# Two-layer decoder on one core: top-k attention in 56 full tiles instead of 64, a laid-out convolution kernel, and gating, norms and biases placed elsewhere

## The chip, the cores and the metric

The kernel runs on one core of one Trainium2 chip, all in float32, in one launch. The time is the device time of the slowest core in microseconds; with one core that is the core's own. TensorE (PE) multiplies matrices, VectorE (DVE), ScalarE (ACT) and GpSimd (POOL) work on rows of up to 128 partitions, and SyncE (SP) issues the transfers. All operands lie in on-chip memory as [partitions x columns]; matmul results go to eight PSUM banks of 2 KB a partition.

## The reference, cut to what matters

The input x is (16, 112, 256), the context (16, 375, 192). Each of six parts is added to x and the sum normalised:

```python
x = _layernorm(x + _L0_attn_ref(x, ...))       # selective scan, 16 sequences of 112
x = _layernorm(x + _L0_xattn_ref(x, ctx, ...)) # softmax cross-attention, 16 heads of 16
x = _layernorm(x + _L0_ffn_ref(x, ...))        # gate, best 2 of 8 experts, 256 -> 256 -> 256
x = _layernorm(x + _L1_attn_ref(x, ...))       # 4 encoder layers over the 16 rows of a position, FFN 1024
x = _layernorm(x + _L1_xattn_ref(x, ctx, ...)) # the part below
x = _layernorm(x + _L1_ffn_ref(x, ...))        # 3 cycles of a coupling network
```

The fifth part is the one that the change touches most (4 heads of 32, K_TOP = 32, here T = 112 rows and G = 375 context positions a batch):

```python
scores = einsum('bthd,bghd->bhtg', Q, K) / sqrt(DH)
scores = where(vision_mask, scores, -inf)
topv, topi = top_k(scores, 32);  probs = softmax(topv)
attn_mean = zeros.at[..., topi].set(probs).mean(axis=1)     # over the 4 heads
c_t = (attn_mean @ V) * text_mask
x = layernorm(x_text, g_norm_in, b_norm_in)
x = x * (1 + gate * scale_in) + gate * shift_in             # both from c_t @ W_film_in
y = causal convolution of x with a kernel of 112 lags for each of 256 features, + D_skip * x
y = y * (1 + gate * scale_out) + gate * shift_out           # both from c_t @ W_film_out
xt = x_text + y;  h = layernorm(xt, g_ffn, b_ffn);  xt = xt + gelu(h @ W1 + b1) @ W2 + b2
return layernorm(xt, g_norm_out, b_norm_out)
```

## The kernel before, in words

Each stage is a set of functions, one for each engine (`xat_pe`, `moe_dve`, `s4x_act` and so on), and each engine runs its functions in the order in which they are written. Semaphores alone tie the engines together, so an instruction that waits holds up everything behind it on its engine. The stages by their start in the trace: selective scan 0 us, cross-attention 333, gating and experts 651, encoder 914, the fifth part 1793, coupling network 2410.

**Cross-attention** (`xat_*`) runs in slots, a pair of heads each: scores L858, exponential, weighted values L871 and L891, and at the end of a batch its sums and its output projection (L901, L910, L919, added to the residual at L1045). Four batches are a quarter; at a quarter's end its rows are normalised (statistics L265 and L268, a root on GpSimd L285, application L277) and turned to features (L936). **Gating** comes after the last quarter: 64 TensorE instructions L1120 for all 16 batches, the two best experts on VectorE (L1196 to L1209), the weights turned at L1126 and copied at L1213. **Experts**: 32 steps (quarter, expert) of hidden L1137 and output L1158, added to the rows at L1224 with the weight of the gate.

**Encoder**: at its start the residual rows are turned back (L1293) in seven rounds, GpSimd adds a bias to each (L1639) and then builds the expanded queries (L1658) for the scores L1349.

**Top-k attention** (`s4x_*`): for each of 16 batches keys L1906, then for each of 4 heads a tile of 112 rows x 375 scores in a PSUM bank: L1917 contracts over the head's 32 features, in rows 32h to 32h+31 of the array, and L1919 adds the mask row with the same 32 rows. VectorE takes tiles in pairs: four rounds of MAX8 (L2158) and MATCH_REPLACE8 (L2167) mark the 32 best, ScalarE has meanwhile made the exponential (L2102), and L2177 keeps the marked ones and sums them. For each batch L2180 and L2181 give 1/sum, ScalarE makes a scaled diagonal of it for each head (dg, L2111), and L1928 multiplies the probabilities by it, which turns them and adds the heads up; L1937 gathers the context, L1946 makes c_t for each quarter. TensorE's order is keys(b+1), scores(b+1), then the context of b.

**Convolution**: the rows are normalised and modulated (L1969 for scale and shift, L2198, L2199), flipped in time by 8 matmuls with a reversed identity (L1983) and copied to x_r (L2118). Then 16 "taps" of 16 features each: 16 Toeplitz matrices of 112 x 112 are read from DRAM (rows of 448 bytes at overlapping addresses of a padded kernel) into 8 buffers (L1856, L1861), and L1996 multiplies each by the rows of 16 batches of one feature (32 columns, two features); L2006 turns the result. Scale and shift out, and the feed-forward part with L2052, follow for each quarter.

Quoted, the lines that set TensorE's order in the top-k stage:

```python
for b in range(B):
    if b + 1 < B:
        keys(b + 1)
        scores(b + 1)
    context(b)
    if b % QB == QB - 1:
        values(b // QB)
```

## Time and profile before

| what | value |
|---|---|
| median of 3 runs | 2531.08 us (2530.32 to 2533.37) |
| the profiled execution's own time | 2530.24 us |
| its span | 2528.4 us |
| mean granted TensorE clock | 0.883 |
| PE, DVE, ACT, POOL busy | 85%, 61%, 28%, 31% |
| chain that ended last, by engine | PE 62%, DVE 22%, POOL 6%, ACT 3% |
| moved by DMA | 101.68 MB, mean 40 GB/s |

The span runs from the first instruction to the last of the core. A program matmul in float32 shows as two instructions in the trace (x4 in a row of the trace are two matmuls of the program). A granted clock of 1.0 is TensorE at 2.4 GHz, 0.5 is 1.2 GHz, and a value between them is a stretch with both. In the program's names wc, wb, XD, XF, enc_w are storage used by several stages, so that a row's name can be that of an earlier owner.

### The profile page before, as it was taken

Reading aid. Unit: us, or ns where it says so; the run is one execution under the profiler, and the core shown is the slowest. Engines: PE = TensorE matmul, PEld = TensorE weight load, DVE = VectorE, ACT = ScalarE, POOL = GpSimd, SP = SyncE. Lnnn points to the kernel's source line nnn. Section 1 sums busy time; section 2 is a strip of 40 time slices with the busy share of each in tenths; the row PEclk is TensorE's granted clock in tenths of the full one; section 3 lists DMA queues with packets and bytes.
Section 4 is the critical chain, followed back from the end, with each engine's and each line's share of the span. In section 5 each row is a group of like instructions: output and inputs, shape, how many; then the busy total and the mean of one; then the engine's idle time right before and its main releaser. Section 6 shows DMA issues by size and latency. Waiting matters only on the chain.

```text
span 2528.4 us, 37624 instructions
## 1 busy us (share of the span) xinstructions
PE 2141.5 (85%) x15316; PEld 1493.9 (59%) x15316; DVE 1547.5 (61%) x3090; ACT 708.1 (28%) x1355; POOL 772.8 (31%) x707
## 2 busy tenths in 40 slices
PE   7888889999799978999999999887667775869886
PEld 2333457777566657878788787775445453336532
DVE  7998845555233325555656565575499896636546
ACT  6544333333112112222222222221222221211132
POOL 3334259876000034433444334332200001201101
PEclk8777789998699989999999999998767676879988
DMA  4212272221100010001001001000421111220001
GB/s 146 86 52 92 87 155 71 59 67 39 54 1 1 1 80 1 1 2 65 1 1 65 1 1 49 1 1 1 106 65 37 28 28 31 48 56 1 0 1 29
DMA packets 63597, 101.68 MB, mean 40 GB/s; under 512 B 32361, under 2 KB 56930, under 8 KB 62210
## 3 DMA queue, kind: packets, MB, share of 16 engines
q1 hardware_dynamic: 63426, 99.28, 13.8%
q8 instruction: 122, 2.00, 0.3%
q14 instruction: 49, 0.40, 0.1%
HBM read 78.77 MB, written 20.50 MB: 39 GB/s over the span
## 4 chain that ended last, share of the span: by engine, by line
PE 62%; DVE 22%; POOL 6%; ACT 3%; issue 3%; SPq 2%; DMA 2%; POOLq 0%; DVEq 0%; ACTq 0%
PE PS L1404 8%; PE PS L1420 8%; PE PS L1158 4%; DVE top L2158 4%; PE PS L1137 3%; DVE w_s L2167 3%; PE PS L1321 3%; PE PS L2043 2%; DVE ln_st L265 2%; PE PS L871 2%; PE PS L858 2%; PE PS L1349 2%; PE PS L1379 2%; PE PS L1431 2%; PE PS L404 2%
## 5 line engine op out<-in xcount | busy, mean ns | idle before, releaser
L284 POOL TENSOR_SCALAR ln_ve<-ln_mv 128x2 f32<-128x2 f32 (+1 forms) x91 | 20.9, 229 | 1309.4 <-DVE ln_mv L268 1309.3
L1596 DVE TENSOR_TENSOR p_x<-PS,cols 128x1024 f32<-128x1024 f32 x112 | 129.3, 1216 | 148.0 <-PE PS L1366 147.9
L1658 POOL TENSOR_TENSOR q_x<-q_f,cols 128x2048 f32<-128x2048 f32 x56 | 208.7, 3746 | 7.7 <-ACT q_f L1516 7.7
L1016 DVE TENSOR_REDUCE XD<-PS 112x2 f32<-112x750 f32 x128 | 120.1, 940 | 112.1 <-PE PS L858 111.9
L1224 DVE SCALAR_TENSOR_TENSOR XA<-PS,gate_w,XA 112x256 f32<-112x256 f32 x128 | 61.9, 484 | 133.7 <-PE PS L1158 133.7
L1928 PE MATMUL PS<-dg,e_p 112*125 112x112 f32 x384 | 82.5, 409 | 70.3 <-ACT dg L2111 70.3
L452 PE MATMUL PS<-bc_parts,ident 96*128 96x448 bf16 x256 | 106.0, 518 | 42.2 <-DVE st_h L686 28.9
L858 PE MATMUL PS<-enc_w,q_s 32*112 32x375 f32 x512 | 132.6, 544 | 4.7 <-DVE XD L1016 4.7
L984 ACT ACTIVATE e_t<-PS 125x672 f32<-125x672 f32 x128 | 93.5, 731 | 152.2 <-PE PS L871 152.2
L1486 ACT ACTIVATE wb<-PS,cols 128x256 f32<-128x256 f32 x224 | 90.8, 472 | 140.1 <-PE PS L1404 140.1
L1928 PEld LDWEIGHTS PS<-dg,e_p 112*125 112x125 f32 x384 | 79.3, 321 | 82.4 <-issue 82.4
L871 PE MATMUL PS<-q_s,enc_w 32*125 32x112 f32 x1536 | 124.2, 293 | 2.6 <-ACT e_t L984 2.6
L642 DVE TENSOR_TENSOR_SCAN st_h<-dA,st_h 128x3584 f32<-128x3584 f32 x16 | 121.0, 7606 | 0.0
L1158 PE MATMUL PS<-wc,h_t 128*112 128x256 f32 x512 | 117.5, 384 | 2.4 <-DVE XA L1227 2.4
L1404 PE MATMUL PS<-wc 128*128 128x256 f32 x448 | 104.4, 393 | 10.3 <-ACT wc L1531 10.3
L1158 PEld LDWEIGHTS PS<-wc,h_t 128*112 128x112 f32 x512 | 91.4, 179 | 32.4 <-issue 14.3
L1404 PE MATMUL PS<-wc,enc_w 128*128 128x256 f32 x448 | 100.4, 382 | 9.5 <-ACT wc L1531 9.5
L871 PEld LDWEIGHTS PS<-q_s,enc_w 32*125 32x125 f32 x1536 | 103.1, 193 | 8.0 <-issue 7.9
L741 POOL TENSOR_TENSOR st_h<-st_h 128x448 f32<-128x448 f32 x64 | 71.2, 1134 | 109.9 <-DVE st_h L686 109.9
L1404 PEld LDWEIGHTS PS<-wc 128*128 128x128 f32 x448 | 86.8, 196 | 26.0 <-ACT wc L1531 14.0
L1137 PE MATMUL PS<-XF,wc 128*128 128x448 f32 x256 | 101.4, 540 | 0.7 <-DVE gate_wt L1213 0.7
L2167 DVE MATCH_REPLACE8 w_s<-top,w_s 112x375 f32<-112x375 f32 x192 | 100.9, 533 | 0.0
(352 smaller groups left out, 4749.7 us busy)
## 6 DMA issues: line engine op xcount, KB each, us to landing
v_all_scratch<-v_st SPq DMA_DIRECT2D x16, 750.0 KB
v_t<-v_all_scratch SPq DMA_DIRECT2D x16, 750.0 KB
t_ring<-k_scratch SPq DMA_DIRECT2D x8, 784.0 KB, 11.9
enc_w<-in_enc_w SPq DMA_DIRECT2D x2, 3072.0 KB, 11.0
wc<-in_enc_w SPq DMA_DIRECT2D x2, 3072.0 KB, 11.5
k_all_scratch<-k_st SPq DMA_DIRECT2D x16, 375.0 KB
enc_w<-k_all_scratch SPq DMA_DIRECT2D x64, 93.8 KB, 3.6
ctx_k<-in_ctx SPq DMA_DIRECT2D x16, 281.2 KB
```

Source lines behind the costliest of these rows:

```text
L642: dve.tensor_tensor_scan(h, dA[:, n, :, :].rearrange("p n b t -> p (n b t)"), h, 0.0, ALU.mult, ALU.add).then_inc(scan_done, 1)
L858: ins = pe.matmul(ps[2 * (n % 2) + a][0:T, 0:S2], q_s[h, m, b * T:(b + 1) * T], k_s[h, b % 3, m, :], start=True, stop=True)
L871: ins = pe.matmul(ps[4 + a][0:JR, j * T:(j + 1) * T], k_s[h, b % 3, m, j * JR:(j + 1) * JR], q_s[h, m, b * T:(b + 1) * T], start=True, sto ...
L1016: dve.tensor_reduce(nm_w[0:T, g % 4, 64 * half + 16:64 * half + 49:32], PS[0:T, 2 * half:2 * half + 2, 0:S2], AX.X, ALU.max, negate=True). ...
L1137: last = pe.matmul(ps[pair + m][:, 0:QT], w1_e[:, e, k, m * P:(m + 1) * P], XF[:, k, q * QT:(q + 1) * QT], start=(k == 0), stop=(k == KC - 1))
L1158: last = pe.matmul(bank, h_t[:, i % 2, k, b * T:(b + 1) * T], w2_e[:, e, k, :], start=(k == 0), stop=(k == KC - 1))
L1404: last = pe.matmul(ps[bank][:, (m % 2) * RT:(m % 2 + 1) * RT], w[:, k, m * P:(m + 1) * P], x1f[:, i % 2, k, :], start=(k == 0), stop=(k == ...
L1420: last = pe.matmul(ps[3][:, g * D:(g + 1) * D], h_ff[:, m, g * P:(g + 1) * P], w[:, m, :], start=(m == 0), stop=(m == 7))
L1596: last = dve.tensor_tensor(p_x[:, m, :, :, :], ps[1][:, m * P:(m + 1) * P].rearrange("p (h i) -> p h i", i=16).unsqueeze(2) .to_broadcast( ...
L1658: last = pool.tensor_tensor(q_x[:, c, :, :].rearrange("p t (h i) -> p t h i", i=16), q_f[:, k % 2, c, :].rearrange("p (t i) -> p t i", i=1 ...
L1928: last = pe.matmul(bank[0:JR, j * T:(j + 1) * T], e_p[:, XH * (b % 2) + h, j * JR:(j + 1) * JR], dg[:, b % 2, h, :], start=(h == 0), stop= ...
L2167: ins = dve.match_replace(w_s[:, a, :], top8[:, a, turn, :], s, FILL)
```

## The change

What it does, by stage:

- **Gating.** The gate products of quarters 0 to 2, the choice of the two experts and the application of the norms become uses of the cross-attention's slots; the last quarter's, the end of batch 15 and all turns of the gate weights go in between the first steps of the experts (`tail(i)`). Norm statistics and their application stand two slots apart. Output banks of the experts hold two batches each. Small weights are loaded earlier.
- **Encoder.** The residual rows are turned behind the first projections, and GpSimd's first biases stand behind its first query products, 2, 2 and 3 at a time.
- **Convolution kernel.** 112 transfers within DRAM write the Toeplitz matrices out once, (T, D, T), 12.8 MB, during the encoder. A tap then reads 7168 bytes in a row for each of 112 partitions, in a time order that needs no flip: the 8 flips and their 8 copies go. The stationary operand is x2[:, :, d], 16 columns at a stride of 256 elements. There are 10 buffers, 6 of them filled early.
- **Norm before the convolution.** Statistics on VectorE before the top-k stage, the rest on GpSimd during it.
- **Top-k.** The 4 heads x 112 rows of a batch are 448 rows; two batches are 896 = 7 tiles of 128. The queries are spread block-diagonally over 128 features x 448 columns (q_z, by ScalarE), so that one matmul over K = 128 gives the scores of 128 rows of heads and tokens. Of 7 tiles one is split 64/64 between two batches. The mask keeps its K = 32 matmul. 56 tiles, 28 steps of two. The diagonals come from a shifted identity.
- **End.** The first four scale-and-shift products stand between the last batch's context steps. GpSimd adds b_out and b2.

TensorE in the middle of the top-k stage before: the last head's scores (L1917) and mask (L1919), then the context of the batch before, then the next keys. Three equal pairs of L1917 and L1919 stand ahead of these rows.

```order
L1917 MATMUL PS<-k_e,q_e 112x375
L1919 MATMUL PS<-mskb,ident 112x375
L1928 MATMUL PS<-dg,e_p 125x112 x12
L1937 MATMUL PS<-at_t,ctx_k 128x112 x3
L1937 MATMUL PS<-at_t,ctx_k 64x112 x3
L1906 MATMUL PS<-ctx_f,enc_w 128x375 x2
```

The same place now (L2078 scores, L2080 mask, L2090 attend, L2100 gather; wa is the new place of at_t): half a split tile and a full tile stand ahead of the context of one batch.

```order
L2078 MATMUL PS<-k_e,q_z 64x375
L2080 MATMUL PS<-mskb,ident 64x375
L2078 MATMUL PS<-k_e,q_z 128x375
L2080 MATMUL PS<-mskb,ident 128x375
L2090 MATMUL PS<-dg,e_p 125x112 x12
L2100 MATMUL PS<-wa,ctx_k 128x112 x3
L2100 MATMUL PS<-wa,ctx_k 64x112 x3
```

The scores went from matmuls over 32 rows of the array to matmuls over all 128, and the masks between them did not. The context's 18 matmuls a batch are the same in number.

TensorE from the cross-attention to the experts before: the end of batch 15, the last turn of rows, all gates, all turns of gate weights, then the first hidden step.

```order
L901 MATMUL PS<-ident,XD 112x4 x4
L910 MATMUL PS<-ident,rs_s 32x112 x16
L919 MATMUL PS<-enc_w,XD 112x256 x4
L936 MATMUL PS<-ident,XA 128x112 x8
L1120 MATMUL PS<-moe_small,XF 112x8 x32
L1126 MATMUL PS<-ident,gate_w 8x112 x16
L1137 MATMUL PS<-XF,wc 128x448 x8
```

Now (L1258 hidden, L1274 and L1280 outputs, L977 a turn of gate weights, L922, L931, L940 the end of batch 15):

```order
L912 MATMUL PS<-e_t,v_t 32x112 x12
L1258 MATMUL PS<-XF,wc 128x448 x4
L912 MATMUL PS<-e_t,v_t 32x112 x12
L977 MATMUL PS<-ident,gate_w 8x112 x4
L1258 MATMUL PS<-XF,wc 128x448 x4
L922 MATMUL PS<-ident,XD 112x4 x4
L1274 MATMUL PS<-moe_b,q_s 112x256 x4
L1280 MATMUL PS<-wc,q_s 112x256 x8
L1258 MATMUL PS<-XF,wc 128x448 x4
L931 MATMUL PS<-ident,rs_s 32x112 x16
L1280 MATMUL PS<-wc,q_s 112x256 x8
```

The first hidden step now stands ahead of the last sums of batch 15, and no gate product of the first three quarters is left here.

GpSimd at the encoder's start before:

```order
L1634 MEMSET k_z 128x32x32
L1635 MEMSET v_z 128x32x32
L1639 TENSOR_TENSOR XA<-xg,enc_rows 128x512 x7
L1658 TENSOR_TENSOR q_x<-q_f,cols 128x2048 x4
L284 TENSOR_SCALAR ln_ve<-ln_mv 128x2
```

And now:

```order
L1768 MEMSET k_z 128x32x32
L1769 MEMSET v_z 128x32x32
L1794 TENSOR_TENSOR q_x<-q_f,cols 128x2048 x2
L1774 TENSOR_TENSOR XA<-xg,enc_rows 128x512 x2
L1794 TENSOR_TENSOR q_x<-q_f,cols 128x2048 x2
```

The query products moved ahead of the seven biases.

The core of the diff:

```diff
-            pe.wait_ge(gate_loaded, 32)
-            pe.wait_ge(xf_ready, 16)
-            for b in range(B):
-                for k in range(KC):
-                    last = pe.matmul(ps[0][0:T, b * E8:(b + 1) * E8], XF[:, k, b * T:(b + 1) * T],
-                                     moe_small[:, k * E8:(k + 1) * E8], start=(k == 0), stop=(k == KC - 1))
-            last.then_inc(gate_ready, 1)
...
+        def kernel_rows(sp):
+            k = dr["k_pad"]
+            sp.wait_ge(k_stored, 16)
+            for t in range(T):
+                lags = bass.AP(tensor=k.tensor, offset=k.offset + T - t, ap=[[2 * T, D], [1, T]])
+                sp.dma_start(dr["k_full"][t], lags).then_inc(k_stored, 16)
...
+                if k == 0:
+                    turn_residuals()
...
+                for r in ((0, 1), (2, 3), (4, 5, 6))[k] if k < 3 else ():
+                    first_bias(r)
...
         def toeplitz(j):
-
-            k = dr["k_pad"]
-            return bass.AP(tensor=k.tensor, offset=k.offset + j * TD * 2 * T + 1,
-                           ap=[[1, T], [2 * T, TD], [1, T]])
+            return dr["k_full"][:, j * TD:(j + 1) * TD, :]
...
+        def tile_parts(n):
+
+            u, r = divmod(n, 7)
+            if r == 3:
+                return [(2 * u, slice(0, 64)), (2 * u + 1, slice(64, P))]
+            return [(2 * u + (r > 3), slice(0, P))]
...
-            def scores(b):
-                pe.wait_ge(m_used, m_count("k", b) + 1)
-                for h in range(XH):
-                    n = XH * b + h
-                    if n >= 4:
-                        pe.wait_ge(x_exp, n - 3)
-                    r = slice(32 * h, 32 * h + 32)
-                    pe.matmul(ps[h][0:T, 0:S2], q_e[r, b * T:(b + 1) * T], k_e[r, b % 2, :],
-                              start=True, stop=False)
-                    pe.matmul(ps[h][0:T, 0:S2], ident[r, 32 * h + b:32 * h + b + 1].to_broadcast([32, T]), mskb[r, :],
-                              start=False, stop=True).then_inc(x_s_ready, 1)
-
-            def context(b):
+            def scores(n):
+                parts = tile_parts(n)
+                pe.wait_ge(m_used, m_count("k", parts[-1][0]) + 1)
+                pe.wait_ge(qz_ready, n // 7 + 1)
+                if n >= 4:
+                    pe.wait_ge(x_exp, n - 3)
+                at, r = P * (n % 7), slice(32 * (n % 4), 32 * (n % 4) + 32)
+                for b, s in parts:
+                    queries = q_z[:, n // 7 % 2, :, :].rearrange("p z m -> p (z m)")[:, at + s.start:at + s.stop]
+                    pe.matmul(ps[n % 4][s, 0:S2], queries, k_e[:, b % 2, :], start=True, stop=False)
+                    row_mask = ident[r, r.start + b:r.start + b + 1].to_broadcast([32, s.stop - s.start])
+                    last = pe.matmul(ps[n % 4][s, 0:S2], row_mask, mskb[r, :], start=False, stop=True)
+                last.then_inc(x_s_ready, 1)
+
+            def attend(b):
 
                 bank = m_claim(pe, "at", b)
-                pe.wait_ge(x_dg, b + 1)
+                pe.wait_ge(x_dg, (first_tile(b) + 3) // 2 + 1)
+                tiles = [(n, s) for n in range(first_tile(b), first_tile(b) + 4) for o, s in tile_parts(n) if o == b]
                 for j in range(JC):
-                    for h in range(XH):
-                        last = pe.matmul(bank[0:JR, j * T:(j + 1) * T],
-                                         e_p[:, XH * (b % 2) + h, j * JR:(j + 1) * JR], dg[:, b % 2, h, :],
-                                         start=(h == 0), stop=(h == XH - 1))
+                    for at, (n, s) in enumerate(tiles):
+                        last = pe.matmul(bank[0:JR, j * T:(j + 1) * T], e_p[s, n % 8, j * JR:(j + 1) * JR],
+                                         dg[s, n % 8, :], start=(at == 0), stop=(at == 3))
                 last.then_inc(m_ready, 1)
+
+            def gather(b):
...
-            for b in range(B):
-                if b + 1 < B:
-                    keys(b + 1)
-                    scores(b + 1)
-                context(b)
-                if b % QB == QB - 1:
-                    values(b // QB)
-
-            pe.wait_ge(x_exp, B * XH)
-            pe.wait_ge(m_used, len(M_AT))
-            pe.wait_ge(e_prep, 5)
+            scores(1)
+            for i in range(STEPS_T):
+                if i + 1 < STEPS_T:
+                    scores(2 * i + 2)
+                    scores(2 * i + 3)
+                for b in finished(i - 1):
+                    attend(b)
+                    gather(b)
+                    if b % QB == QB - 1:
+                        values(b // QB)
+                for b in keys_at(i):
+                    keys(b)
 
             def film(b, side, used, ready):
...
-            for b in range(B + 2):
-                if b < B:
-                    film(b, 0, fi_used, fi_ready)
-                if b >= 3 and b % 2 == 1:
-                    i = (b - 3) // 2
-                    pe.wait_ge(x2_ready, 2 * i + 2)
-                    if i >= 4:
-                        pe.wait_ge(conv_copied, i - 3)
-                    pe.matmul(ps[2 + i % 4][0:T, :], flip, x2[:, 2 * i:2 * i + 2, :].rearrange("t b d -> t (b d)"),
-                              start=True, stop=True).then_inc(conv_ready, 1)
-
-            pe.wait_ge(conv_copied, FLIPS)
+            pe.wait_ge(x_exp, TILES)
+            pe.wait_ge(e_prep, 5)
+            film(0, 0, fi_used, fi_ready)
+            film(1, 0, fi_used, fi_ready)
+            attend(B - 1)
+            film(2, 0, fi_used, fi_ready)
+            gather(B - 1)
+            film(3, 0, fi_used, fi_ready)
+            values(NQ - 1)
+            for b in range(4, B):
+                film(b, 0, fi_used, fi_ready)
+            pe.wait_ge(x2_ready, B)
...
-                    wide = 2 if d + 1 < D else 1
-                    last = pe.matmul(ps[2 + j % 4][32 * g:32 * g + B * wide, slot * T:(slot + 1) * T],
-                                     x_r[:, d:d + wide, :].rearrange("t d b -> t (d b)"), t_slots[j % SLOTS_T][:, i, :],
-                                     start=True, stop=True)
+                    last = pe.matmul(ps[2 + j % 4][32 * g:32 * g + B, slot * T:(slot + 1) * T],
+                                     x2[:, :, d], t_slots[j % SLOTS_T][:, i, :], start=True, stop=True)
...
+            def spread_queries(u):
+                if u >= 2:
+                    act.wait_ge(x_s_ready, 7 * (u - 1))
+                for h in range(XH):
+                    r = slice(32 * h, 32 * h + 32)
+                    last = act.copy(q_z[r, u % 2, :, h * T:(h + 1) * T],
+                                    q_e[r, 2 * u * T:2 * (u + 1) * T].rearrange("p (z t) -> p z t", t=T))
+                last.then_inc(qz_ready, 1)
...
+                    if n >= 8:
+                        act.wait_ge(m_ready, m_count("at", tile_parts(n - 8)[-1][0]) + 1)
+                    act.activation(e_p[:, n % 8, :], ps[n % 4][:, 0:S2], ACT.Exp,
+                                   bias=neg_m[:, n % 4:n % 4 + 1]).then_inc(x_exp, 1)
```

## Rows read from the trace of the kernel before

**Rows 1.** The page, busy time by engine over the whole span.
```profile
PE 2141.5 (85%) x15316; PEld 1493.9 (59%) x15316; DVE 1547.5 (61%) x3090; ACT 708.1 (28%) x1355; POOL 772.8 (31%) x707
```

**Rows 2.** Windows: stretch and length, busy (instructions) by engine, granted clock, DMA share, GB/s.
```profile
1810.61:2116.71 306.10, 203.81 (x864) 144.57 (x864) 293.15 (x992) 74.41 (x190) 5.27 (x6) 0.69 0.20 52
2116.71:2198.74 82.03, 60.34 (x124) 25.96 (x124) 49.13 (x96) 11.32 (x17) 23.78 (x16) 0.74 0.08 20
2198.74:2235.22 36.48, 29.29 (x577) 22.26 (x577) 9.73 (x16) 8.51 (x16) 0.00 (x0) 0.81 0.84 178
```

**Rows 3.** VectorE's waits in 1850 to 2116: us in total, times, longest.
```profile
DVE e_p L2177 <- ACT e_p L2102: 9.5, 2, 5.2
```

**Rows 4.** Timeline of TensorE, 1884 to 1922: start, us, then the idle time before.
```profile
1899.14 3.83 PE L1946 MATMUL PS<-XD,enc_w 128*128 128x448 f32 x8 [0.57 <-ACT XD L2087]
1902.90 1.72 PE L1906 MATMUL PS<-ctx_f,enc_w 128*128 128x375 f32 x4
...
1909.47 4.48 PE L1928 MATMUL PS<-dg,e_p 112*125 112x112 f32 x24 [1.84 <-ACT dg L2111]
1914.53 1.61 PE L1937 MATMUL PS<-at_t,ctx_k 125*128 125x112 f32 x12 [0.57 <-ACT at_t L2081]
```

**Rows 5.** Timeline of TensorE, 1956 to 1996.
```profile
1970.58 2.90 PE L1937 MATMUL PS<-at_t,ctx_k 125*128 125x112 f32 x12 [0.57 <-ACT at_t L2081]
...
1981.19 3.16 PE L1906 MATMUL PS<-ctx_f,enc_w 128*128 128x375 f32 x4
1984.92 2.06 PE L1917 MATMUL PS<-k_e,q_e 32*112 32x375 f32 x7 [0.56 <-ACT k_e L2078]
...
1986.78 1.91 PE L1919 MATMUL PS<-mskb,ident 32*112 32x375 f32 x6
1988.62 5.38 PE L1928 MATMUL PS<-dg,e_p 112*125 112x112 f32 x24
```

**Rows 6.** Windows, columns as in rows 2: two stretches inside the top-k stage.
```profile
1900.00:1905.00 5.00, 4.62 (x11) 1.48 (x10) 5.00 (x16) 1.41 (x3) 0.00 (x0) 1.00 0.42 114
...
1977.00:1995.00 18.00, 16.86 (x51) 10.02 (x51) 11.88 (x41) 5.23 (x12) 0.00 (x0) 0.50 0.05 13
```

**Rows 7.** Line L1906 (keys): what TensorE waited for, us and times.
```profile
  DMA ctx_f<-in_ctxT: 9.2, 2
```

**Rows 8.** Timeline of TensorE, 2116 to 2140.
```profile
2118.09 5.35 PE L1928 MATMUL PS<-dg,e_p 112*125 112x112 f32 x24 [11.10 <-ACT dg L2111]
...
2127.49 7.20 PE L1946 MATMUL PS<-XD,enc_w 128*128 128x448 f32 x8 [0.57 <-ACT XD L2087]
...
2135.36 4.81 PE L1969 MATMUL PS<-enc_w,c_t 128*112 128x512 f32 x7 [0.67 <-issue]
```

**Rows 9.** Timeline of TensorE in the convolution, 2194 to 2240.
```profile
2217.51 0.97 PE L1996 MATMUL PS<-t_ring,x_r 112*32 112x112 f32 x32 [1.99 <-DMA t_ring<-k_scratch]
```

**Rows 10.** Timeline of TensorE, 650 to 693: from the first layer's attention to its experts.
```profile
656.88 3.45 PE L919 MATMUL PS<-enc_w,XD 128*112 128x256 f32 x8 [0.83 <-DVE XD L1039]
...
670.73 12.12 PE L1120 MATMUL PS<-moe_small,XF 128*112 128x8 f32 x64 [2.46 <-DMA moe_b<-in_moe_b]
687.96 3.15 PE L1126 MATMUL PS<-ident,gate_w 112*8 112x112 f32 x16 [5.11 <-DVE gate_w L1209]
691.81 1.39 PE L1137 MATMUL PS<-XF,wc 128*128 128x448 f32 x3 [0.70 <-DVE gate_wt L1213]
```

**Rows 11.** TensorE's waits in 386 to 651: us in total, times, longest.
```profile
PE PS L841 <- DVE q_s L1023: 9.4, 2, 5.8
PE PS L858 <- DVE XD L1016: 3.5, 1, 3.5
```

**Rows 12.** Timeline of TensorE at a quarter's end among the experts, 744 to 760.
```profile
754.61 3.68 PE L1158 MATMUL PS<-wc,h_t 128*112 128x256 f32 x16 [0.85 <-DVE XA L1227]
```

**Rows 13.** Timeline of TensorE at the encoder's start, 910 to 945.
```profile
943.21 2.15 PE L1349 MATMUL PS<-q_x,k_z 128*32 128x128 f32 x36 [8.63 <-POOL q_x L1658]
```

**Rows 14.** Timeline of TensorE in the feed-forward part, 2302 to 2318.
```profile
2308.93 1.53 PE L2052 MATMUL PS<-ident,XA 112*128 112x112 f32 x8 [2.52 <-DVE XA L277]
```

More of the change, by code:

```diff
@@ L960, in xat_pe @@
                     weigh((n - 3) // 2)
+            return tail
         def xat_act(act):
@@ new lines, in add_row, with best_two @@
+            def add_row(b):
+                dve.wait_ge(wo_ready, b + 1)
+                if b == 0:
+                    dve.wait_ge(res_biased, 8)
+                dve.tensor_tensor(XA[0:T, b, :], xat_bank("wo", b)[0:T, 0:D], XA[0:T, b, :], ALU.add)\
+                    .then_inc(wo_added, 1)
+            def best_two(q):
+                dve.wait_ge(gate_ready, q + 1)
+                dve.tensor_tensor(gate_s[0:T, :, 0:E8],
+                                  xat_bank("gate", q)[0:T, 0:QB * E8].rearrange("p (b e) -> p b e", e=E8),
+                                  row("moe_bg", T).unsqueeze(1).to_broadcast([T, QB, E8]), ALU.add)\
+                    .then_inc(gate_added, 1)
+                dve.wait_ge(gate_added, q + 1)
+                for i in range(QB):
+                    last = dve.max(gate_m[0:T, i, :], gate_s[0:T, i, :])
+                link(last)
+                link(dve.tensor_copy(gate_p[0:T, :, 0:2], gate_m[0:T, :, 0:2]))
@@ L1025, in xat_dve, with rows_of, apply_rows @@
+            def rows_of(q):
+                return [XA[0:T, q * QB + i, :] for i in range(QB)]
+            def apply_rows(q, stats):
+                for i, x in enumerate(rows_of(q)):
+                    last = norm_apply(dve, stats, i, x, x)
+                last.then_inc(norm_done, 1)
             for n in SLOTS:
@@ L2184, in s4x_dve @@
[L2184 to L2192 removed]
+            for q in range(NQ):
+                dve.wait_ge(xa_copied, 2 * (q + 1))
+                norm_stats(dve, link, [XA[0:T, q * QB + i, :] for i in range(QB)])
```

565 lines of the change are left out of this document (333 added, 232 removed).

## Prediction, made before the changed kernel ran

> **What bounds the kernel now.** I read the page's busy times first, then windows cut at the stages' borders, then the waits inside each stage, and last the timeline of the waits that were found. Over the whole span TensorE is busy for 85% [rows 1], but the stages differ, and the change touches four kinds of place.
>
> In the top-k stage, 306.1 us from the first MAX8 to the last sum, VectorE is busy for 293.15 us and TensorE for 203.8 [rows 2]. VectorE sets the pace here: of its 13 idle us, 9.5 are two waits for an exponential [rows 3]. TensorE's reserve is smaller than its busy share says. The granted clock is 0.69 as a mean over the stage [rows 2]; the reader should see that this is a mixture, with 1.00 in one stretch and 0.50 in another, where TensorE is busy for 16.9 of 18 us and VectorE only for 11.9 [rows 6]. There TensorE is the bound already.
>
> Between the top-k stage and the convolution, 82 us, neither engine is full (60 and 49 us busy), since scale-and-shift, modulation, norm, flips and copies wait for one another. The convolution, 36.5 us, has a DMA share of 0.84 and waits for its matrices [rows 2, 9]. From the cross-attention to the experts TensorE stands or does small work from 656.9 to 691.8 us [rows 10].
>
> **Top-k on VectorE.** I take an instruction over 128 rows and 375 columns to cost what one over 112 rows and as many columns does, so 56 tiles cost 56/64 of 64: 293.15/64 = 4.58 us a tile [rows 2], 56 x 4.58 = 256.5. Reciprocals come 28 times instead of 16; with them I take 260. That 33 us comes back only where VectorE stays the bound.
>
> **Top-k on TensorE.** I add up four batches, which are 14 tiles now. A full tile is two matmuls of 375 columns, score and mask, one after the other. The nearest row is the keys' pair, as wide: 1.72 us at full clock, 3.16 at half [rows 4, 5]. A split tile is two such pairs, and 2 of 14 are split: 16 pairs, 27.5 or 50.6 us. The context keeps its 18 matmuls a batch: 4.48 and 1.61 us at the higher clock, 5.38 and 2.90 at the lower. Four keys are 6.9 or 12.6, the values of a quarter 3.83 [rows 4] or 7.20 [rows 8], and five round trips to ScalarE of 0.57 are 2.9. The sums are 27.5 + 17.9 + 6.4 + 6.9 + 3.8 + 2.9 = 65.5 us at full clock and 50.6 + 21.5 + 11.6 + 12.6 + 7.2 + 2.9 = 106.4 at half. VectorE needs 260/4 = 65 for the same four batches. Before, at half clock, a batch's scores and masks took 3.8 us (1984.92 to the end at 1988.69) [rows 5], 15 for four batches where the tiles now take 50.6; the total was 15 + 21.5 + 11.6 + 12.6 + 7.2 + 5.2 = 73, against VectorE's 73. So at full clock the two engines are now level; at half clock TensorE needs 41 us more than VectorE for each four batches.
>
> The reason is in those rows. Before, the 8 matmuls of a batch stood in four different groups of 32 rows and ran side by side: 3.8 us for 8, where each alone takes about 1.6. Now the scores fill all 128 rows and can share the array with nothing, and the mask still costs a full pass. The Trainium skill states the rule on the page "TensorE: Matmul & The Clock Gate", Part 3 on packing small matmuls: one matmul over K = 32 takes as long as one over K = 128, and four in distinct row groups ran 3.07 times as fast as one after another. By that ratio the 12.6 us of 8 would be 4.1; the trace has 3.8 and agrees. The page "TensorEngine Tiling (Array Packing)", Key Properties, adds that a change of tiling mode drains TensorE; each tile now has two such changes. No row here isolates that price, and I add nothing for it.
>
> The clock decides. I take the mixture of the stage before, 0.69, which is 62% of the time at half: the rate is 0.38/65.5 + 0.62/106.4 = 0.01163 a us, so 86 us for four batches and 344 for the stage. Behind that come the last step's VectorE work with nothing beside it, 9 us, and the waits for ctx_f. The transfer for batch b+1 is issued only after the context of b-2 was gathered, and the keys now follow that directly at three places a stage; a wait was 4.6 us [rows 7], so 13. The stage takes 366: **+60 us**. The ends are 278 (VectorE bound, 260 and 18 of waits at quarter ends and behind exponentials that stand in ScalarE's queue behind the values' copies), -28, and 426 + 9 = 435, +129. I keep the value by the mixture, since it is the stage's own.
>
> The stage's entry: keys(1) and its DMA wait of 4.6 now stand ahead of the first scores, and ScalarE makes the first spread queries there: **+7** (0 to +10).
>
> **End of top-k to convolution**, 82.0 now. The chain: 1.4 to the first context matmul [rows 8], 5.4, 0.6, 2.9, 0.6, 7.2, 0.6, and two scale-and-shift products of 4 instructions at 0.69 in between, which cover round trips: 4.3 more, 23 in all. Twelve products are left, 48 instructions at 0.43 (full) or 0.69 [rows 8], 21 or 33; the norm is done on GpSimd during top-k, and flips and copies are gone. The last modulation adds 1.5. I take 45: **-37** (-45 with all at full clock, -22 with all at half).
>
> **Convolution**, 36.5: TensorE is busy for 29.3 at a mean clock of 0.81 [rows 2], some 24 at full clock, if no matrix is late. Runs of 7168 bytes instead of 448 and ten buffers instead of eight make that likely, and I take a stationary operand of 16 columns to cost no more than one of 32: **-12** (-14 to 0; the strided operand could slow the weight load, for which no row stands). Writing the matrices, 12.8 MB in 112 transfers, lies in the encoder, over 850 us long and nearly without DMA. I cost it at nothing; if a layer's weights were late behind it, some 10 us.
>
> **From cross-attention to experts.** From the end of the last slot (651.4) to the first hidden step (691.8) are 40 us. What comes back between the experts' steps: 3.45 for L919, some 3 for the sums before it, 2 for the last turns, a quarter of L1120's 12.12, and 3.15 for L1126 [rows 10]: 14.6, and 3 of new waits. **-23** (-31 to -16). The other three quarters of L1120, 9.1 us at that clock, go into slots, which are bound by TensorE. In return the waits behind the norms, 9.4 and 3.5 us [rows 11], should go, since statistics and application stand two slots apart: **-4** (-12 to +5).
>
> **The small ones.** Each quarter's end among the experts waits 0.85 for the rows [rows 12], and the output banks hold two batches: -3. At the encoder's start TensorE waits 8.63 us for query products that stand behind seven biases [rows 13]; they now stand ahead: -8. In the feed-forward part the bias additions leave VectorE, and the wait of 2.52 [rows 14] at each quarter should halve: -5. Together **-16** (-22 to -6).
>
> **Sum.** 60 + 7 - 37 - 12 - 23 - 4 - 16 = -25. The profiled execution took 2530.24 us, of which 2528.4 is its span, and lies 0.8 below the median. So 2531 - 25 = **2506 us**.
>
> **The rivals.**
>
> *VectorE stays the bound.* TensorE is granted full clock for most of the stage: its gaps shrink, and its work is now mostly over 128 rows. For it: the clock is 1.00 in a stretch where TensorE worked for 4.6 of 5 us [rows 6]. Against it: it was 0.50 where TensorE worked for 16.9 of 18. The stage takes 278, and the sum is -28 + 7 - 45 - 12 - 23 - 4 - 16 = -121: 2410 us.
>
> *TensorE at half clock throughout (slower).* Once TensorE falls to 1.2 GHz in the top-k stage it needs 106 us for four batches, is never idle, and nothing in the rows says that being busy brings the clock back; 18 us of it did not [rows 6]. Masks over 32 rows take as long as the scores while they use a quarter of the array. The stage takes up to 435; the sum is 129 + 7 - 30 - 12 - 23 - 4 - 16 = +51, and with a fifth of the stage at full clock about +33: 2564. It decides from a stage of 306 + 85 = 391 us, that is 92 us for four batches, a mean clock of about 0.62 instead of 0.69.
>
> *The rest does not deliver.* The clock is as before, but the gates in the slots cost more than they free (the slots are bound by TensorE and its order), and the convolution keeps its waits: half of the 92 us of the other terms. 2531 + 60 - 42 = 2549.
>
> **How the numbers follow.** The mixed clock 0.46, VectorE as the bound 0.20, half clock 0.24, the rest failing 0.10. The likeliest gives 2506. Its own range is 2465 to 2540. The range for 8 in 10 reaches to the other cases: 2410 to 2562. A measurement of this kernel tells 0.2%, 5 us, from no change. Faster by more: 0.44 of the first case, all of the second, 0.02 of the others: 0.66. Within it: 0.06. Slower: 0.28.
>
> **What the profile would show.** The top-k stage: its length from first MAX8 to last sum, TensorE's busy share, and the granted clock. If I am right, VectorE waits for L2080 (masks) in most steps where the clock is 0.5, and TensorE no longer waits for the diagonals; with the clock at 1.0 the step is 9.3 us. Between the last sum and the first convolution matmul 45 us, the convolution 24 without DMA waits, the first hidden step some 37 us earlier relative to the last slot, with the remaining work among the first experts' steps. The prediction is wrong if VectorE is busy for over 95% of the stage, if the stage exceeds 391 us, or if a DMA wait appears at the encoder's layers or the convolution.

## The result, and the profile after

The changed kernel takes 2570.4 us (2563.97 to 2574.25, 4 runs) against 2532.2 (2530.32 to 2536.31): a ratio of 1.0146, 95% interval 1.012 to 1.0172. It is **slower by 1.5%**. The forecast was 2506 with a range of 2410 to 2562. The profiled execution took 2568.31 us at a span of 2565.5, which is 37.1 above the span before.

Stage by stage, from the starts of the same instructions in both traces, in us. The forecasts are the prediction's terms.

| stretch | before | after | change | forecast |
|---|---|---|---|---|
| up to the queries' projection (L1898, now L2057) | 1800.7 | 1756.9 | -43.8 | -23 - 4 and -11 of the small ones |
| projection to first MAX8 | 9.9 | 20.2 | +10.3 | +7 |
| top-k, first MAX8 to last sum | 306.1 | 443.4 | **+137.3** | +60 |
| last sum to first convolution matmul | 82.0 | 37.1 | -44.9 | -37 |
| convolution | 36.5 | 30.5 | -6.0 | -12 |
| to the end of the feed-forward part | 175.7 | 162.4 | -13.3 | -5 |
| rest | 117.5 | 114.9 | -2.6 | 0 |

All that is not the top-k stage brought 100 us where 85 were forecast. The top-k stage alone ate it, and 37 more. These windows of the changed kernel answer to [rows 2] (same columns; the third ends with the last tap, 2.4 us before the next stage):

```profile
1777.10:2220.50 443.40, 392.12 (x879) 190.05 (x880) 266.35 (x868) 73.06 (x199) 41.68 (x32) 0.52 0.12 30
2220.50:2257.60 37.10, 34.11 (x102) 15.22 (x100) 25.91 (x50) 2.56 (x7) 0.00 (x0) 1.00 0.31 87
2257.60:2285.80 28.20, 24.60 (x566) 19.18 (x568) 8.61 (x14) 8.36 (x15) 0.00 (x0) 0.94 0.64 173
```

VectorE's own work did shrink, from 293.15 to 266.35 us, near the 260 forecast. But TensorE's went from 203.8 to 392.1 at a granted clock of 0.52 where it was 0.69. The slices of the page show how steady that is (40 slices of 64 us; the 28th to 35th cover the stage):

```profile
PE   7988889999999789999999998877889888979986
PEclk7777789998999899999999999986555555789998
```

What VectorE waited for in the stage, against [rows 3]: 9.5 us for exponentials before, now 108.6, and 63.6 for masks that TensorE had not yet written (before, 1.7 in the window of rows 3).

```profile
DVE e_p L2353 <- ACT e_p L2279: 108.6, 16, 13.3
DVE top L2334 <- PE PS L2080: 63.6, 28, 5.2
```

The exponential stands in ScalarE's queue behind the copies of context and keys, and ScalarE waits for TensorE at these: most likely the same cause under another name. ScalarE's waits for TensorE in the stage:

```profile
ACT wa L2258 <- PE PS L2090: 175.6, 16, 14.2
ACT k_e L2255 <- PE PS L2065: 115.8, 14, 14.9
```

A step of TensorE at the low clock, from its timeline, answers to [rows 5]:

```profile
1939.07 2.91 PE L2100 MATMUL PS<-wa,ctx_k 125*128 125x112 f32 x12 [0.57 <-ACT wa L2258]
1941.90 1.62 PE L2078 MATMUL PS<-k_e,q_z 128*128 128x375 f32 x2
1943.45 1.61 PE L2080 MATMUL PS<-mskb,ident 32*128 32x375 f32 x2
1945.00 1.62 PE L2078 MATMUL PS<-k_e,q_z 128*128 128x375 f32 x2
1946.55 1.62 PE L2080 MATMUL PS<-mskb,ident 32*128 32x375 f32 x2
```

Matmuls of scores and masks start 1.55 us apart, 3.10 a tile. The forecast took 3.16 from the keys. So the tiles' price at half clock was right; what was wrong is how much of the time is spent at it. And TensorE, now the bound, still waits for a transfer, 38.3 us in 8 waits (32.3 in 6 of them inside the stage, the others at its entry), where two waits made 9.2 us in [rows 7]:

```profile
1877.35 2.91 PE L2100 MATMUL PS<-wa,ctx_k 125*128 125x112 f32 x12 [0.57 <-ACT wa L2258]
1886.48 3.13 PE L2065 MATMUL PS<-ctx_f,enc_w 128*128 128x375 f32 x4 [6.22 <-DMA ctx_f<-in_ctxT]
```

The transfer was issued at 1880.60, behind the gather that had ended at 1880.26, for keys that are next in TensorE's order.

Such waits do more than hold TensorE up. In the stage TensorE reached full clock three times, at 1853.5, 2061.8 and 2208.5 (read in slices of 0.25 us), and the first two times it lost it again 3.5 us later, at 1857.0 and 2065.2, inside the next wait for ctx_f:

```profile
1858.73 3.13 PE L2065 MATMUL PS<-ctx_f,enc_w 128*128 128x375 f32 x4 [2.27 <-DMA ctx_f<-in_ctxT]
...
2066.88 3.14 PE L2065 MATMUL PS<-ctx_f,enc_w 128*128 128x375 f32 x4 [2.66 <-DMA ctx_f<-in_ctxT]
```

Between them lie 205 us at half clock, of which TensorE worked for 181:

```profile
1857.00:2062.00 205.00, 181.22 (x399) 89.33 (x400) 112.11 (x366) 35.08 (x96) 0.00 (x0) 0.50 0.07 18
```

### The profile page after: what moved, and what is told of

Its sections match the earlier page's. It is cut to its first block, busy times and chain, and to the rows that moved or that the text cites. A ratio compares the mean times of both kernels' runs of the same rounds, so it can differ in the third digit from the quotient of the medians.

```text
span 2565.5 us, 37680 instructions
## 1 busy us (share of the span) xinstructions
PE 2287.6 (89%) x15300; PEld 1516.2 (59%) x15300; DVE 1499.2 (58%) x2955; ACT 703.8 (27%) x1367; POOL 811.1 (32%) x730
## 4 chain that ended last, share of the span: by engine, by line
PE 76%; DVE 11%; POOL 5%; ACT 3%; DMA 3%; issue 2%; SPq 1%; POOLq 0%; DVEq 0%; ACTq 0%
PE PS L1531 8%; PE PS L1547 8%; PE PS L1280 4%; PE PS L2090 4%; PE PS L1258 4%; PE PS L1448 4%; PE PS L2078 3%; PE PS L2080 3%; DMA ctx_f<-in_ctxT 2%; PE PS L2205 2%; PE PS L2195 2%; PE PS L892 2%; PE PS L2134 2%; PE PS L879 2%; PE PS L1476 2%
## 5 line engine op out<-in xcount | busy, mean ns | idle before, releaser
L1337 DVE SCALAR_TENSOR_TENSOR XA<-PS,gate_w,XA 112x256 f32<-112x256 f32 x128 | 56.0, 479 | 125.6 <-PE PS L1280 125.6
L1280 PE MATMUL PS<-wc,q_s 128*112 128x256 f32 x512 | 116.0, 380 | 0.3
L2078 PE MATMUL PS<-k_e,q_z 128*128 128x375 f32 (+1 forms) x128 | 99.1, 876 | 8.4 <-issue 6.1
L1280 PEld LDWEIGHTS PS<-wc,q_s 128*112 128x112 f32 x512 | 89.7, 177 | 26.9 <-issue 9.1
L1531 PEld LDWEIGHTS PS<-wc 128*128 128x128 f32 x448 | 87.6, 198 | 26.5 <-ACT wc L1665 14.0
L2090 PE MATMUL PS<-dg,e_p 128*125 128x112 f32 (+1 forms) x384 | 101.5, 429 | 0.4 <-ACT dg L2291 0.4
L1258 PE MATMUL PS<-XF,wc 128*128 128x448 f32 x256 | 101.6, 540 | 0.0
L2090 PEld LDWEIGHTS PS<-dg,e_p 128*125 128x125 f32 (+1 forms) x384 | 82.7, 302 | 31.6 <-issue 30.5
```

The costliest lines, as they stand in the source:

```text
L1258: last = pe.matmul(ps[pair + m][:, 0:QT], w1_e[:, e, k, m * P:(m + 1) * P], XF[:, k, q * QT:(q + 1) * QT], start=(k == 0), stop=(k == KC - 1))
L1280: last = pe.matmul(bank, h_t[:, i % 2, k, b * T:(b + 1) * T], w2_e[:, e, k, :], start=(k == 0), stop=(k == KC - 1))
L1531: last = pe.matmul(ps[bank][:, (m % 2) * RT:(m % 2 + 1) * RT], w[:, k, m * P:(m + 1) * P], x1f[:, i % 2, k, :], start=(k == 0), stop=(k == ...
L2078: pe.matmul(ps[n % 4][s, 0:S2], queries, k_e[:, b % 2, :], start=True, stop=False)
L2090: last = pe.matmul(bank[0:JR, j * T:(j + 1) * T], e_p[s, n % 8, j * JR:(j + 1) * JR], dg[s, n % 8, :], start=(at == 0), stop=(at == 3))
```

## The experiments

All are the changed kernel with one to three edits (e1 puts a whole stage back). Times are medians of four runs. The other columns are of the one profiled run, which lies 15 us below the median in g2 (2453.0) and 11 in e3 (2439.7): "stage" is the top-k stage as above, "clock" its granted clock, "longest at half" its longest stretch at half clock (read in slices of 1 us). The kernel before has 306.1, 0.69, 9.2 and 38 there.

| run | us | ratio to before (95%) | stage | clock | waits for ctx_f | longest at half |
|---|---|---|---|---|---|---|
| changed kernel | 2570.4 | 1.0146 (1.012 to 1.0172) | 443.4 | 0.52 | 38.3 | 205 |
| e1 old top-k stage | 2422.5 | 0.9563 (0.9543 to 0.9584) | 313.0 | 0.65 | 7.4 | 51 |
| e2 masks over 128 rows | 2441.2 | 0.9642 (0.9621 to 0.9663) | 313.4 | 0.81 | 67.3 | 24 |
| e3 no masks | 2450.5 | 0.9669 (0.9632 to 0.9705) | 314.1 | 0.71 | 78.3 | 27 |
| e4 ctx_f early | 2468.6 | 0.9739 (0.972 to 0.9759) | 348.1 | 0.66 | 1.7 | 99 |
| g1 masks over 64 rows | 2565.3 | 1.012 (1.0097 to 1.0143) | 439.8 | 0.52 | 35.7 | 165 |
| g2 e4 with masks over 64 rows | 2468.3 | 0.9748 (0.9727 to 0.977) | 339.6 | 0.68 | 1.7 | 99 |
| f4 e4 with masks side by side | 2418.5 | 0.956 (0.9529 to 0.9592) | 289.7 | 0.75 | 2.0 | 41 |
| f1 e2 and e4 together | 2393.6 | 0.9453 (0.943 to 0.9476) | 269.8 | 0.85 | 2.6 | 14 |
| f2 f1 with masks in bf16 | 2394.6 | 0.946 (0.943 to 0.949) | 269.5 | 0.78 | 2.0 | 21 |
| f3 f2 with keys(1) later | 2387.6 | 0.9426 (0.94 to 0.9453) | 270.1 | 0.78 | 2.5 | 20 |

My theory was that the new tiles alone cost the time, since TensorE is at half clock and their matmuls run one after another. The first rival was that the parts moved around the stage cost some of it.

**e1: the top-k stage as before, all else changed.**

```diff
-            def scores(n):                       # 56 tiles, K = 128
+            def scores(b):                       # 64 tiles of 112 rows, K = 32 in four row groups
...
-                for b in finished(i - 1):
-                    attend(b)
+                    keys(b + 1)
+                    scores(b + 1)
+                    attend(b)
```

> All parts of the change but the top-k stage, which is as before again: 64 tiles of 112 rows, scores over 32 rows of the array in four row groups. Theory (the new tiles alone cost the time, since their scores and masks run one after the other at TensorE's half clock): the stage is back at some 306 us instead of 443, so 2570 - 137 = 2433 us (2420 to 2445). Rival (what was moved around the stage, GpSimd's norm and the new kernel matrices, costs part of it): above 2460 us, with a top-k stage well over 306.

Measured: 2422.5, stage 313.0. The rival falls: what was put beside the stage, GpSimd's norm above all, costs at most 313 - 306 = 7 us. The loss lies in the new tiles, 130 us in the stage and 10 at its entry; why they cost it, this run does not say. Its window:

```profile
1765.90:2078.90 313.00, 220.72 (x872) 152.91 (x872) 298.81 (x991) 74.38 (x190) 51.12 (x40) 0.65 0.19 50
```

**e2: the mask matmuls contract over 128 rows instead of 32.**

```diff
-                    row_mask = ident[r, r.start + b:r.start + b + 1].to_broadcast([32, s.stop - s.start])
-                    last = pe.matmul(ps[n % 4][s, 0:S2], row_mask, mskb[r, :], start=False, stop=True)
+                    row_mask = ident[:, r.start + b:r.start + b + 1].to_broadcast([P, s.stop - s.start])
+                    last = pe.matmul(ps[n % 4][s, 0:S2], row_mask, mskb[:, :], start=False, stop=True)
```

> The changed kernel; each mask matmul contracts over all 128 rows of the array instead of 32 (the same column count, the same result; the other rows add zero). Theory A (the half clock comes from matmuls that fill a quarter of the rows): the granted clock rises above 0.8 in the top-k stage, the stage falls from 443 to 280 to 310 us, total 2410 to 2440. Theory B (TensorE stays at 1.2 GHz whatever rows the mask uses): clock 0.5, stage 440, total 2565 to 2575. If only a drain between row modes is saved, some 5 to 15 us at clock 0.5.

Measured: 2441.2, clock 0.81, stage 313.4: 1 and 3 us above the ranges of theory A and far from theory B, from an edit that takes no instruction away.

```profile
1776.70:2090.10 313.40, 226.88 (x866) 129.73 (x864) 269.04 (x868) 73.49 (x197) 44.71 (x33) 0.81 0.17 44
```

But the timeline shows a second thing that differs. At half clock the matmuls now start 1.25 us apart instead of 1.55 (1808.59 to 1809.84), and at full clock 0.63 (1817.91 to 1818.54) instead of 0.83 in the changed kernel (1854.74 to 1855.57):

```profile
1808.59 1.46 PE L2078 MATMUL PS<-k_e,q_z 128*128 128x375 f32 x2
1809.84 1.08 PE L2080 MATMUL PS<-mskb,ident 128*128 128x375 f32 x2
...
1817.91 0.79 PE L2078 MATMUL PS<-k_e,q_z 128*128 128x375 f32 x2
1818.54 0.79 PE L2080 MATMUL PS<-mskb,ident 128*128 128x375 f32 x2
```

```profile
1854.74 0.90 PE L2078 MATMUL PS<-k_e,q_z 128*128 128x375 f32 x2
1855.57 0.89 PE L2080 MATMUL PS<-mskb,ident 32*128 32x375 f32 x2
```

So next to a matmul over 32 rows each of the two starts 0.30 us later at half clock and 0.20 at full; this text calls it the pause. With 128 score and mask matmuls that is 38 or 26 us. Was it the number of rows in a mask, or the alternation, that held the clock down? g1 and g2 below ask this.

**e3: no masks at all** (leaves out the masking of context positions).

```diff
-                    last = pe.matmul(ps[n % 4][s, 0:S2], row_mask, mskb[r, :], start=False, stop=True)
```

> The changed kernel without the mask matmuls of the top-k stage (leaves out the masking of context positions). Half of the tiles' TensorE work goes: four batches need 106 - 25 = 81 us at half clock, 52 at full, and VectorE 65. Theory A (masks keep the clock down): clock above 0.8, VectorE the bound, stage 270 to 290 us, total 2400 to 2420. Theory B (clock stays at half): 4 x 81 = 325 and some 30 of DMA waits, stage 350, total 2475 to 2490.

Measured: 2450.5, clock 0.71, stage 314.1. Neither expectation: with the masks gone it is not clearly faster or slower than e2, which kept them all (runs of 2439.7 to 2457.9 against 2440.0 to 2449.2). Both are held up by the same wait, 78.3 and 67.3 us for ctx_f. In e2 one of these lasts 19.6 us:

```profile
1802.86 3.13 PE L2065 MATMUL PS<-ctx_f,enc_w 128*128 128x375 f32 x4 [19.57 <-DMA ctx_f<-in_ctxT]
```

This longest one has a cause of its own. The transfer for batch 2 was issued behind six convolution matrices of 784 KB each, and the DMA engines were full (share 1.02) while TensorE stood still:

```profile
1768.25 2.54 SPq L1993 DMA_DIRECT2D t_ring<-k_full_scratch  x4
...
1771.79 0.94 SPq L1983 DMA_DIRECT2D ctx_f<-in_ctxT  x2
```

```profile
1785.00:1790.00 5.00, 0.00 (x0) 0.00 (x0) 4.86 (x13) 0.67 (x2) 4.73 (x5) 0.65 1.02 239
```

**e4: ctx_f of batch b+1 is issued as soon as the keys of b-1 are done.**

```diff
+            context_features(0)
             for b in range(B):
-                if b >= 2:
-                    sp.wait_ge(m_ready, m_count("k", b - 2) + 1)
-                for i in range(2):
-                    sp.dma_start(ctx_f[0:CR[i], b % 2, i, :], ...)
+                if b + 1 < B:
+                    context_features(b + 1)      # waits for the keys of b - 1
                 if b >= 2:
                     sp.wait_ge(m_ready, m_count("m1", b - 2) + 1)
```

> The changed kernel; the transfer of ctx_f for batch b+1 is issued as soon as the keys of b-1 are done, ahead of the wait for the context of b-2. The 38 us that TensorE waits for ctx_f (8 times) should fall to some 6. Theory (TensorE is the bound, so each wait is lost time): total falls by 25 to 32 us, to 2538 to 2545, and the clock stays at 0.5. Rival (the waits lie beside VectorE's work): within 8 us of 2570.

Measured: 2468.6, which is 102 us less, nearly three times what the waits held. The waits fell from 38.3 to 1.7, but the clock also rose, from 0.52 to 0.66. My expectation that it stays at 0.5 was wrong. The edit does two things at once: it takes the issue out from behind the gathers, and it moves batch 2's transfer ahead of the convolution matrices (1768.59, the matrices from 1771.02 on). Without the waits a stretch at full clock lasts, 55 us from 1859 on, where the two above lasted 3.5. A stretch at half clock lasts too: 99 us, with TensorE at work for 95.6 of them:

```profile
1859.00:1914.00 55.00, 49.71 (x190) 24.41 (x190) 46.16 (x153) 17.80 (x47) 0.00 (x0) 1.00 0.15 42
2009.00:2108.00 99.00, 95.56 (x219) 48.23 (x218) 62.50 (x204) 15.44 (x44) 0.00 (x0) 0.50 0.05 15
```

Two stretches of 20 us, one at each level:

```profile
1880.00:1900.00 20.00, 18.48 (x70) 8.73 (x69) 19.73 (x65) 8.00 (x21) 0.00 (x0) 1.00 0.11 30
...
2040.00:2060.00 20.00, 18.85 (x37) 8.17 (x36) 5.50 (x20) 3.39 (x9) 0.00 (x0) 0.50 0.11 29
```

TensorE is busy for 18.5 and 18.9 of 20 us in them, but gets through 70 instructions in the one and 37 in the other. VectorE's busy time falls from 19.7 to 5.5. A busy share alone does not say what TensorE delivers.

**g1 and g2: masks over 64 rows**, in the changed kernel and in e4.

```diff
-                    row_mask = ident[r, r.start + b:r.start + b + 1].to_broadcast([32, s.stop - s.start])
+                    r64 = slice(64 * (n % 2), 64 * (n % 2) + 64)
+                    row_mask = ident[r64, r64.start + b:r64.start + b + 1].to_broadcast([64, s.stop - s.start])
```

> The changed kernel with mask matmuls over 64 rows of the array (32 before this edit, 128 in the wide-mask run). Matmuls of scores and masks started 1.55 us apart at half clock and 0.83 at full in the changed kernel, 1.25 and 0.64 with masks over 128 rows: a change between row counts costs 0.2 to 0.3 us. With 64 rows the change is still there. If the wide masks helped by sparing this change, this run is like the changed kernel: clock 0.50 to 0.55, stage 435 to 445, total 2560 to 2575, starts 1.55 and 0.83 apart. If they helped by bringing the clock up, the clock rises here too, to 0.6 to 0.8, with starts still 1.55 and 0.83 apart: stage 330 to 400, total 2455 to 2530.

> The same edit on the kernel with ctx_f issued early (2469 us, stage 348, clock 0.66; with masks over 128 rows 2394, 270, 0.85). If the change between row counts is what costs: 2460 to 2470 and clock 0.66. If the rows count for the clock: clock 0.72 to 0.85, stage 280 to 320, total 2400 to 2440.

Measured: 2565.3 at clock 0.52, and 2468.3 at 0.68. Doubling the rows did nothing that the medians show (the runs overlap with those of the changed kernel and of e4). The starts are 1.55 apart, as expected:

```profile
1846.20 1.62 PE L2078 MATMUL PS<-k_e,q_z 128*128 128x375 f32 x2
1847.75 1.62 PE L2081 MATMUL PS<-mskb,ident 64*128 64x375 f32 x2
```

This speaks against what I wrote for e2 ("matmuls that fill a quarter of the rows"): twice the rows changed nothing while the pause stayed. The pause at each change of row count, 0.2 to 0.3 us, is shown, and where the change between scores and masks is gone the clock comes back sooner. The last column of the table tells it apart from the waits: e4 and g2 wait for ctx_f as little as f1 (1.7 against 2.6 us) and still stay at half clock for up to 99 us, f1 for 14 at most. Whether the pause itself holds the clock down, or a number of mask rows between 64 and 128 decides, these runs do not separate.

**f4: masks of a step's two tiles behind both scores, in different row groups** (with e4's edit).

```diff
+                masks = [(n, b, s) for n in pair for b, s in tile_parts(n)]
+                for k, (n, b, s) in enumerate(masks):
+                    g = (2 * (n // 2) + k) % 4
+                    r = slice(32 * g, 32 * g + 32)
```

> As the kernel with ctx_f early (2469 us, stage 348), but the masks of the two tiles of a step stand behind both tiles' scores, in different groups of 32 rows, in float32. If passes in different row groups run side by side here as in the kernel before, a step saves one mask pass, 1.6 us at half clock, 28 times: TensorE's 323 busy us fall to 285 to 300 and the stage to 310 to 330, total 2430 to 2450. If they do not run side by side: 2465 to 2475.

Measured: 2418.5, stage 289.7, clock 0.75, more than expected. The two masks do run side by side, 4 instructions in 0.90 us, where one mask alone took 0.89 at full clock:

```profile
1895.61 2.20 PE L2084 MATMUL PS<-k_e,q_z 128*128 128x375 f32 x4
1897.73 0.90 PE L2090 MATMUL PS<-mskb,ident 32*128 32x375 f32 x4
```

A whole pass is spared in each step, and half the changes between score and mask.

**f1: e2 and e4 together**; its diff is the two above.

> Both edits together: mask matmuls over all 128 rows and ctx_f issued early. With the mask edit alone TensorE waited 67 us for ctx_f in a stage of 313 us. Theory (that was the last thing that held VectorE up): the waits go, the clock is above 0.85, VectorE is the bound at 270 to 280 us, total 2398 to 2408. Rival (without the waits TensorE's work at a mixed clock becomes the bound): stage above 290 us, total above 2418.

Measured: 2393.6, stage 269.8, clock 0.85. VectorE is busy for 265.25 of 269.8 us: it is the bound, and this is the stage that the 56 tiles were to give:

```profile
1770.60:2040.40 269.80, 220.25 (x866) 138.64 (x864) 265.25 (x868) 76.48 (x197) 50.84 (x40) 0.85 0.22 59
```

**f2: f1 with the mask in bf16.**

```diff
-        mskb = sb("mskb", [P, S2], pool=s4a)
+        mskb = sb("mskb", [P, S2], BF16, pool=s4a)
...
+                    row_mask = ident16[:, b:b + 1].to_broadcast([P, s.stop - s.start])
```

> As the run before it, with the mask row and its selector in bf16 (mask values 0 and minus 1e30; the sum stays in the same float32 bank), over all 128 rows: a mask pass should take a quarter of the float32 one. Theory (VectorE is the bound already): within 8 us of the run before it. Rival (TensorE is still part of the bound): 8 to 15 us faster. A third outcome: with less work TensorE has more gaps, the clock falls below 0.75, and the stage is longer, as without the masks (314 us).

Measured: 2394.6, the same as f1. TensorE's busy time falls by 14 us, its clock to 0.78, and the stage stays at 269.5, with VectorE busy for 265.4: it is the bound.

**f3: f2 with keys(1) behind the first two tiles.**

```diff
             keys(0)
-            keys(1)
             scores(0)
             scores(1)
+            keys(1)
```

> As the run before it, with keys(1) behind the scores of the first two tiles, which need only batch 0. The first MAX8 should come 5 to 8 us earlier after the queries (it was 20 us after them in the changed kernel, 10 before the change), total 5 to 8 us less. If the second batch's keys are then late for the third tile, no gain.

Measured: 2387.6, 7 us less than f2 by the medians, as expected, but not for the reason expected. From the projection to the first MAX8 it is 12.1 us (1753.28 to 1765.41), against 20.2 in the changed kernel; but f2 already had 12.6 there (and e4 12.9), since its second keys no longer wait for their transfer. So the new place of keys(1) gives 0.5 us at the entry, the two profiled spans differ by 2.7 us, and the stage is not shorter (270.1 against 269.5): where the 7 us come from is not shown, and f2's runs reach from 2391.1 to 2402.9. One of f3's four runs took 6487 us, the others 2386.5 to 2388.6; nothing here explains that one. Leaving it aside, this is the fastest version, 0.9426 (0.94 to 0.9453) of the kernel before.

## Why the prediction was wrong

**The step that failed** is "The clock decides. I take the mixture of the stage before, 0.69." It was 0.52. With the prediction's own price at half clock the stage was 4 x 106.4 + 9 = 435 us, and 443.4 was measured; with the mixture it was 366. The mechanism, the level engines at full clock and TensorE's 41 us too many at half, was right, and stood as the rival "TensorE at half clock throughout", with 2564 us and a chance of 0.24. The measured time is 6 us above that and 8 above the range. The prediction's own sign of being wrong, a stage over 391 us, came true. That the time lies so near the rival's is in part luck: its stage was some 417 us (435, less 18 for a fifth at full clock) where 443.4 was measured, and the other parts brought 100 us where it had 78.

Why the old mixture could not be carried over is what the runs add. The clock of a stage is not a property of the stage. It answers to how TensorE's work is cut: taking away the waits for ctx_f (e4) or the alternation of row counts (e2) moved it from 0.52 to 0.66 and 0.81 with as many matmuls. The change brought the alternation in and made four times as much of the waits. Before, TensorE at half clock needed for four batches what VectorE needed, 73 us by the prediction's own sum, so a low clock cost little; now each stretch at it is paid in full.

**The waits for ctx_f** were a second mis-sized term: 13 us forecast for the stage, 32.3 measured in it. I had counted three places of close issue and a wait of 4.6 at each; there are 6, the longest of 9.1 us while the convolution matrices filled the DMA engines. And their price was not their length: with the entry 38 us of waits cost 102, and the clock fell in them.

**The context's products** were priced too high at full clock and too low at half. The 24 instructions of 4.48 us in [rows 4] are no price at full clock: their own stretch has 0.63. The new kernel's take 3.74 at full clock and 6.71 at half, where the forecast had 4.48 and 5.38. The 5.38 was right for the old kernel; the new one's products stand on 128 and 64 rows in turn, and whether that makes the difference is not shown. At half clock it is 5.3 us more for four batches.

```profile
1909.40:1914.00 4.60, 4.48 (x24) 4.33 (x24) 4.60 (x15) 1.10 (x3) 0.00 (x0) 0.63 0.00 0
```

```profile
1813.54 6.71 PE L2090 MATMUL PS<-dg,e_p 128*125 128x112 f32 x24
...
2211.70 3.74 PE L2090 MATMUL PS<-dg,e_p 128*125 128x112 f32 x24 [0.16 <-ACT dg L2291]
```

**The change of row count** I had priced at nothing ("No row here isolates that price"). The Trainium skill's page "TensorEngine Tiling (Array Packing)", Key Properties, says that a change of tiling mode drains TensorE; the runs agree, with 0.20 us at full and 0.30 at half clock for each matmul (e2 against the changed kernel). It did not make the sum wrong by itself, since the keys' pair of 3.16 us [rows 5], which alternates 128 and 64 rows, carries such a pause too (1.55 us from start to start for score and mask, 1.58 for each of the keys). It did hide the cheap repair: e2's edit of two lines is worth 129 us.

**VectorE's saving** was right: 266.35 us busy, forecast 260, and a stage of 269.8 once TensorE keeps up (f1), below the 278 taken as its best.

**Side by side.** The rule of the four row groups, told in the prediction with 3.8 us for 8 matmuls, held in f4 as well, for two.

**The entry** was +10.3 for +7: the second keys waited 4.30 us for their transfer and then ran at half clock, 3.14 us, ahead of the first scores. Issuing their transfer earlier took 7.3 us of it back (e4, 12.9 where it was 20.2).

**End of top-k to convolution**: 37.1 for a forecast of 45, the case "all at full clock" (37.1 at clock 1.00). Flips and norm are gone from it, and the clock is 1.00 where it was 0.74; what each of the two is worth is not separated.

**Convolution**: -6.0 for -12. No wait for a matrix is left, and the 16 strided columns cost next to nothing: taps start 1.51 us apart (2259.94, 2261.45) where 1.49 was the pitch before. But TensorE stands idle for 7.7 us before taps, in 16 gaps for which the profile names no cause, and a stretch near the end still ran at half clock, with 2.35 us idle before it:

```profile
2259.94 1.00 PE L2159 MATMUL PS<-t_ring,x 112*16 112x112 f32 x32
...
2261.45 1.01 PE L2159 MATMUL PS<-t_ring,x 112*16 112x112 f32 x32
...
2279.30 0.77 PE L2159 MATMUL PS<-t_ring,x 112*16 112x112 f32 x19 [2.35 <-issue]
...
2280.84 1.74 PE L2159 MATMUL PS<-t_ring,x 112*16 112x112 f32 x32
```

**From attention to experts and the encoder**: -43.8 for -38. The first hidden step comes at 646.77 instead of 691.81, and the wait for VectorE's q_s is 1.4 us where it was 9.4 [rows 11]; some 5 of these 45 us go to the work that now lies among the experts' steps. The rows, against [rows 10]:

```profile
646.77 3.27 PE L1258 MATMUL PS<-XF,wc 128*128 128x448 f32 x8
649.98 0.78 PE L912 MATMUL PS<-e_t,v_t 125*32 125x112 f32 x24
650.69 0.55 PE L977 MATMUL PS<-ident,gate_w 112*8 112x112 f32 x4
```

At the encoder's start the bias additions no longer stand ahead, and the scores begin 43.5 us earlier; before them TensorE now waits 6.65 us for the transfer of enc_rows. From the end of the experts to the first scores it is 26.5 us where it was 29.5, so 3 of the 8 us forecast for this place came.

**Feed-forward**: -13.3 for -5. A quarter takes 35.51 us (2347.06 to 2382.57) instead of 39.94; the waits of 2.52 are gone altogether, where I had them halved.

**One sum of the rivals** does not come out: for "the rest does not deliver" half of the 92 us named, with +7 of the entry, gives 2552 and not 2549. Nothing else hangs on it.

## What to carry to other kernels

Before a change adds work to an engine that is not the bound, add that work up at both clock levels, and if the sum at the low level exceeds the bound, take the low level as a likely case, not the stage's old mean: here the stage ran at 0.52. Keep neighbouring matmuls at the same row count, or group those of another: a matmul over 32 rows between matmuls over 128 is dearer than one over 128. And when TensorE becomes the bound, look first at the transfers that wait for its own last step or stand behind bulk transfers: here their order in the queue was worth 102 us, and together with the row count it turned a kernel 1.5% slower into one 5.5% faster.

## What the runs showed of the hardware that I had not expected

A mask matmul over 128 rows, three quarters of them with nothing to add, is cheaper between scores over 128 rows than one over 32: 0.63 against 0.83 us at full clock, 1.25 against 1.55 at half. Being busy did not bring the clock back: TensorE worked for 95.6 of 99 us at half clock in e4, where masks over 32 rows alternate with scores over 128, while f1, with the masks at 128, was never at half for more than 14 us. Fewer matmuls did not mean less time: without the masks the kernel took 2450.5 us, with wide masks 2441.2, and the runs of the two overlap. And the granted clock multiplied what was removed: 38 us of waits were worth 102 us, 26 to 38 us of pauses 129.
